# A transformer sandwich kernel: the adapter stage's normalisations moved from VectorE to ScalarE and GpSimd

## What is computed

```python
def _L1_ffn_ref(x, W, b, A, B, p_scores):
    z = jnp.einsum('bsd,od->bso', x, W) + b
    u = jnp.einsum('bsd,edr->ebsr', x, A)
    m = jnp.einsum('ebsr,ero,e->bso', u, B, p_scores)
    norm_z = jnp.linalg.norm(z, axis=-1, keepdims=True)
    norm_m = jnp.linalg.norm(m, axis=-1, keepdims=True)
    gamma = jnp.minimum(C_CLAMP * norm_z / (norm_m + EPS), 1.0)
    return z + gamma * m
...
x = x + _layernorm(_L1_ffn_ref(_layernorm(x, axis=-1), L1_ffn_W, L1_ffn_b, L1_ffn_A, L1_ffn_B, L1_ffn_p_scores), axis=-1)
```

## Time and profile before

| | us |
|---|---|
| median of 3 runs | 2067.3 (2067.06 to 2076.23) |
| profiled execution | 2061.47 |
| its span | 2059.7 |
| PE busy in the span | 1906.8 |
| DVE busy | 1405.4 |
| ACT busy | 1161.7 |
| POOL busy | 233.2 |

### The profile page before, as it was taken

How to read it: one execution, slowest core, us unless ns; L and a number is a source line. 1 busy time by engine, 2 the same in 40 slices (tenths; PEclk the granted TensorE clock), 3 DMA queues, 4 the chain that set the end, 5 groups by cost and what they waited for, 6 DMA issues and landing times. The chain is left out here.

```text
span 2059.7 us, 31844 instructions
## 1 busy us (share of the span) xinstructions
PE 1906.8 (93%) x11664; PEld 1079.1 (52%) x11664; DVE 1405.4 (68%) x2438; ACT 1161.7 (56%) x2422; POOL 233.2 (11%) x284
## 2 busy tenths in 40 slices
PE   6999999999999999989999999399999999999784
PEld 4875333333333333368888888264444444444563
DVE  5346999999998999465334231567777777773677
ACT  3223878888887888744222221124777777776443
POOL 0000000110000000250011010100001110003513
PEclk9999999999999999999999999699999999999998
DMA  6592454435444451143010100463534543431201
GB/s 210 159 194 77 69 83 86 77 70 88 75 74 64 77 84 37 39 139 111 1 41 1 42 21 0 138 172 81 96 100 85 103 86 75 87 70 44 78 21 61
DMA packets 124572, 165.60 MB, mean 80 GB/s; under 512 B 49364, under 2 KB 59988, under 8 KB 124272
## 3 DMA queue, kind: packets, MB, share of 16 engines
q1 hardware_dynamic: 120080, 148.64, 33.0%
q0 software_dynamic: 4336, 14.93, 2.3%
HBM read 104.92 MB, written 58.06 MB: 79 GB/s over the span
## 5 line engine op out<-in xcount | busy, mean ns | idle before, releaser
L961 DVE TENSOR_REDUCE maxesB<-banksB 128x1 f32<-128x1024 f32 x512 | 601.6, 1215 | 86.7 <-PE banksB L1028 86.7
L911 ACT ACTIVATE probsB<-banksB 128x512 f32<-128x512 f32 x1024 | 529.6, 602 | 128.4 <-PE banksB L1039 128.2
L958 DVE CUSTOM_DVE_ANT_0 junkG<-banksG,rampG 128x896 bf16<-128x896 f32 (+7 forms) x512 | 367.7, 755 | 100.5 <-PE banksG L1028 94.7
L1039 PE MATMUL banksB<-q_stackB,k_stackB 50*128 50x512 f32 x1024 | 403.5, 471 | 4.4 <-ACT probsB L911 2.1
L911 ACT ACTIVATE probsG<-banksG 128x512 f32<-128x512 f32 (+3 forms) x768 | 326.0, 492 | 117.2 <-PE banksG L1050 65.7
L1028 PE MATMUL banksB<-k_stackB,q_stackB 48*128 48x512 f32 x1024 | 344.6, 442 | 4.0
L1039 PEld LDWEIGHTS banksB<-q_stackB,k_stackB 50*128 50x128 f32 x1024 | 166.8, 184 | 265.0 <-ACT probsB L911 231.3
L1039 PE MATMUL banksG<-q_stackG,k_stackG 54*128 54x512 f32 (+3 forms) x768 | 258.8, 413 | 22.0 <-ACT probsG L911 16.5
L1072 PE MATMUL banksB<-probsB,v_onesB 128*32 128x512 f32 x2048 | 274.2, 608 | 0.0
L1028 PE MATMUL banksG<-k_stackG,q_stackG 52*128 52x512 f32 (+3 forms) x768 | 247.9, 408 | 8.7 <-DVE maxesG L958 8.3
L1028 PEld LDWEIGHTS banksB<-k_stackB,q_stackB 48*128 48x128 f32 x1024 | 153.9, 185 | 86.0 <-DVE maxesB L961 75.1
(11 more groups left out here) (296 smaller groups left out, 2785.0 us busy)
## 6 DMA issues: line engine op xcount, KB each, us to landing
q_stackB<-q_parts SPq DMA_DIRECT2D x96, 128.0 KB
k_stackB<-k_parts SPq DMA_DIRECT2D x96, 128.0 KB
q_stackG<-q_parts SPq DMA_DIRECT2D x96, 128.0 KB
q_parts<-partsA SPq DMA_DIRECT2D x16, 512.0 KB, 4.0
k_parts<-partsA SPq DMA_DIRECT2D x16, 512.0 KB, 2.8
turns<-o_copyB SPq DMA_DIRECT2D x32, 256.0 KB, 2.2
q_parts<-partsF SPq DMA_DIRECT2D x16, 512.0 KB, 2.8
turns<-o_copyG SPq DMA_DIRECT2D x32, 256.0 KB, 3.1
```

What stands on the lines that cost most here:

```text
L911: act.activation(probs[:, (i % ring) * GH + h, first:HALF], st_ps[:, n % n_st, first:HALF], ACT.Exp).then_inc(st_used, 1)
L958: dve.tensor_tensor_reduce(junk[:, n % JUNK, 0:width], scores, ramp[:, SEQ - width:SEQ], 1.0, LOWEST, ALU.add, ALU.max, out).then_inc(maxe ...
L961: dve.reduce_max(out, scores, AX.X).then_inc(maxed, 1)
L1039: ins = pe.matmul(st_ps[:, n % n_st, first:HALF], kst[at, it % 3, h % kh, kt * P:(kt + 1) * P], qst[at, it % 3, half, h % GS, first:HALF], ...
```

## The change

Three things move, all in the adapter stage. The next block's normalisation goes from VectorE to ScalarE, as `Identity(rstd * x + shift)`; VectorE works out `shift = -mean * rstd` in one small operation; ScalarE does tiles 0 and 1 ahead of the block's tile loop and tiles 2 and 3 behind tile 0. The normalisation of the last block's result goes from VectorE to GpSimd, ahead of its adds, for blocks 0 to 2; block 3's stays on VectorE. VectorE waits for those normalisations before it writes new means.

```diff
@@ block_residual_stats
     dve.wait_ge(r.summed, TB * (nb + 1))
+    if nb:
+        dve.wait_ge(r.normed, TB * nb)
...
 def block_residual_apply(dve, r, nb):
-
+    block_residual_inverse(dve, r, nb)
+    block_residual_tiles(dve, r, nb)
+
+
+def block_residual_inverse(dve, r, nb):
     dve.wait_ge(r.rooted, nb + 1)
     dve.reciprocal(r.rstd[:, :], r.rstd[:, :]).then_inc(r.inverted, 1)
-    dve.wait_ge(r.inverted, nb + 1)
+
+
+def block_residual_tiles(engine, r, nb):
+    engine.wait_ge(r.inverted, nb + 1)
     for i in range(TB):
-        dve.tensor_scalar(r.tile(nb, i), r.tile(nb, i), r.mv[:, i, 0:1], r.rstd[:, i:i + 1],
+        engine.tensor_scalar(r.tile(nb, i), r.tile(nb, i), r.mv[:, i, 0:1], r.rstd[:, i:i + 1],
                           ALU.subtract, ALU.mult).then_inc(r.normed, 1)
@@ Adapter
     def gpsimd(self, pool, out):
         for nb in range(NB):
+            if nb < NB - 1:
+                block_residual_tiles(pool, self.r, nb)
             block_residual_add(pool, self.r, self.n, nb)
+
+    def norm_next(self, act, nb, tiles):
+
+        n = self.n
+        act.wait_ge(n.inverted, nb + 1)
+        act.wait_ge(n.turned, TB * nb)
+        for i in tiles:
+            act.activation(n.xn[:, i, :], n.block(nb)[:, i, :], ACT.Identity, bias=self.shift[:, i:i + 1],
+                           scale=n.rstd[:, i:i + 1]).then_inc(n.normed, 1)
@@ Adapter.scalar
                 norm_root(act, n, nb + 1)
+                self.norm_next(act, nb + 1, range(0, 2))
...
+                if i == 0 and nb < NB - 1:
+                    self.norm_next(act, nb + 1, range(2, TB))
@@ Adapter.vector
             if nb < NB - 1:
-                norm_apply(dve, n, nb + 1)
+                dve.wait_ge(n.rooted, nb + 2)
+                dve.reciprocal(n.rstd[:, :], n.rstd[:, :]).then_inc(self.inverse, 1)
+                dve.wait_ge(self.inverse, nb + 1)
+                dve.scalar_tensor_tensor(out=self.shift[:, :], in0=n.mv[:, :, 0], scalar=-1.0, in1=n.rstd[:, :],
+                                         op0=ALU.mult, op1=ALU.mult).then_inc(n.inverted, 1)
...
                 if i == 3 and nb:
-                    block_residual_apply(dve, r, nb - 1)
+                    block_residual_inverse(dve, r, nb - 1)
```

More of the change, by code:

```diff
@@ L1591, in __init__ @@
         self.shift = slack_sb(f"shift{tag}", [P, TB], F32)
+        self.inverse = sems("ln_inverse")
         self.w = Weights(lambda name, *a: (turn_sb if name.startswith("w_") else slack_sb)(name, *a), sems, tag,
```

## The result

The changed kernel takes 2080.88 us (median of 20 runs, 2072.82 to 2086.89) against 2069.63 us before (20 runs, 2059.84 to 2082.63): a ratio of 1.0046, 95% interval 1.0030 to 1.0062. That is 9.5 us by the ratio and 11.25 us between the medians, and above the forecast range of 2063 to 2078. The profiled execution has a span of 2081.8 us.

The account below looks back on a forecast made before the run. VectorE was taken as the adapter stage's busiest engine, its normalisations and once GpSimd's adds on the path. The terms -1.25 + 2.25 + 2.1 = +3.1 us, put on the median of 2067.3, gave 2070.4 us, range 2063 to 2078.

Parts of the forecast that it names:

- I take 0.80 us: GpSimd in the adapter stage: one normalisation of a tile was taken to cost 0.80 us.
- the bounds of 0.60 and 1.29: Range for GpSimd's normalisation: cast of a tile 0.60 us below, fastest two-input add 1.29 us above.
- the second rival: GpSimd's normalisation costs much more than an add, over 1.43 us; at 2.0 us +17, 2084 us; chance 0.08.
- I to Z: Statistics-ending reciprocal I(b) to first bias add Z(b+2), b the block: 9.5 us (was 9.62), then 9.27 (7.02), including 0.7 and 0.5 lost.
- I(0): Reciprocal ending block 0's statistics: expected at 1994.03 instead of 1995.18 us, with ScalarE's normalisations costed at nothing.
- Z to I stays 14.9: Block 2, first bias add to the next reciprocal ending a result's statistics: unchanged at 14.9 us.
- The last stretch: After I(2), block 3's reciprocal: joins and GpSimd's adds take turns, last statistics at about I + 11.4 against 9.27, +2.1 us.
- the first rival: Last stretch: joins are not held by GpSimd and end at I + 5.7; sum -2.6 us, 2063 to 2065; chance 0.10.
- The wait on y_normed: VectorE's new wait before writing means: met by older work, in the last block by GpSimd's normalisations at I + 3.7.
- MODIFY_POOL_CONFIG: New operation before GpSimd's first normalisation: lies in GpSimd's idle time until after block 0's reciprocal, so costs nothing.
- The third rival: Loading GpSimd's code is paid at block 0's first normalisation: 2071.7 us, or 2076.4 by the skill; chance 0.07.
- own slope of 11.5: Each 0.1 us more per GpSimd normalisation costs 0.4 at Z(2), 0.4 at Z(3), about 0.35 at the end.

Follow-up runs that it names:

- prices: The kernel before plus seven scratch operations run twice on GpSimd in its idle time as the adapter stage starts; stage 109.26 us against 105.75, one run.
- act_only: The changed kernel with the last result's normalisation left on VectorE, so only ScalarE's part moves; ratio to the kernel before 0.9989 (0.9965 to 1.0012).
- pool_only: The changed kernel with the next block's normalisation left on VectorE, so only GpSimd's part moves; ratio to the kernel before 1.0067 (1.0042 to 1.0093).
- three_tiles: The changed kernel with a third buffer for y, so the first bias add waits for older adds; ratio to the kernel before 1.0021 (1.0003 to 1.0039).
- act_three: act_only with a third buffer for the blocks' results; ratio to the kernel before 0.9985 (0.9965 to 1.0004).
- double_stats: The changed kernel with a second buffer for the result's means and roots; adapter stage 119.28 us against 118.94 in the changed kernel, one run.
- beside: The kernel before plus scratch adds, TENSOR_SCALARs or copies on GpSimd beside VectorE's joins, by block; adapter stage 114.45 us against 105.75, one run.

## Why the prediction was wrong

**The step that failed** is the term "I take 0.80 us" in what GpSimd gets and its price, and with it the bounds of 0.60 and 1.29. Measured: 2.08 us. The case stood there as the second rival, "at 2.0 us it is 3.1 + 13.8 = +17, 2084", with a chance of 0.08. It happened, at 2080.9; that this is near 2084 is in part luck, since the growth was 11.25 us and not 17, from a median before of 2069.6 and not 2067.3. What misled was the argument "with one tensor input it is nearer to the cast": prices shows a one-input tensor_scalar of one step at 1.50 us, above the two-input add at 1.30. Of the two reasons weighed in that rival, the pointers ("for it") turn out to be worth 0.1 or 0.2 us; the kind of operation, which wasn't weighed, makes the price. The Trainium skill, GPSIMD Engine Reference, has in section 3.1, Elementwise — side-by-side cycle accounting, 769 ns for 512 elements as the best of a tight loop; the shortest tensor_scalar here took 1499 ns. The upper bound was also no bound: an add is a different operation, so its duration bounds nothing from above.

**I to Z.** The mechanism was right (Z released by GpSimd's adds, one queue of four normalisations and four adds). By its own formula with 2.08 us and no loss to VectorE, 0.33 + 8.3 + 5.14 + 0.1 is 13.9 us, measured 13.60 and 13.56. The 0.7 and 0.5 us for VectorE's operations in between were not lost by GpSimd: its normalisations took 8.29 us for four and its adds 4.96. Here it was VectorE that waited, L1735 1.13 and 1.08 us instead of 0.69.

**ScalarE's part and I(0).** Right to 0.01 us for I(0) in the change (40.07 from the start, 40.08 forecast), and nothing of it showed on the path: act_only.

**Z to I stays 14.9.** It became 16.25, by matmuls at the lower clock level behind TensorE's waits. This 1.34 us was not in the sum. What cost it were the slow transposes and matmuls behind the wait of 3.04 us for the low parts: from the first transpose to the fourth bias add 5.36 us. pool_only, with an equally late Z and a wait of 3.08 us there, had the full clock behind it, took 4.01 us for the same and kept 14.90. three_tiles and act_only had slow matmuls that cost time, act_three had none. What decides the clock is open.

**The last stretch.** +2.49 against +2.1 forecast, a hit by number and not by mechanism. The joins, to be held to about I + 11.4, were done at I(2) + 6.0, as the first rival had it. They met normalisations and not adds, since at 2.08 us each GpSimd was not yet at its adds; beside shows that the one holds joins hardly and the other does. The time was lost in GpSimd's own queue instead: 9.66 us of normalisations, one stretched to 3.49, and then eight adds in a row, 10.52 us.

**The wait on y_normed** was said to be met in the last block by normalisations done at I + 3.7. They were done at I(2) + 9.9, and VectorE waited 1.56 us, yet double_stats shows that this costs nothing. For the results of blocks 1 and 2 it was met, as forecast. **MODIFY_POOL_CONFIG** ran at 1965.6, and 37.56 us of idle time followed: hidden, as forecast. The third rival did not come: GpSimd started 0.27 us after I(0), and in prices it started within 0.2 us of MODIFY_POOL_CONFIG itself. The Trainium skill, GPSIMD Engine Reference, section 2.1, Instruction dispatch, has some 6 us for a first call to new code; the rows of prices do not agree, with 0.2 us and a first operation of 2.10 us.

**Sum.** With 2.08 us the prediction's own slope of 11.5 gives 3.1 + 14.7 = +17.8; the stage grew by 13.19. Of the 4.6 us between, 4.1 are the last stretch, where each 0.1 us was to cost 0.35 but the joins went free; 1.0 and 0.8 are the two I to Z pieces (14.6 and 14.4 by that slope); the slow matmuls take 1.3 back. The prediction's sums at its bounds are slightly off its own slope: it gives +0.8 us at 0.60 and not +0.6, +8.7 at 1.29 and not +8.6, -4.2 and not -4.4 for the first rival at 0.60, and 0.4 less and not 0.3 at 769 ns; nothing hangs on this. The median grew by 11.25 us, and the interval reaches to 12.8; the stage of the one profile of before had no slow matmul and was likely on the short side, which is not shown by more profiles of it.

## What to carry to other kernels

An engine with idle time is not a cheap engine: before an operation is moved to GpSimd, measure that very operation there, by kind and steps, since a cast and an add of the same tile say little about it. When two stages of work share a queue and a third waits for its end, the buffer count and the unit of the wait matter as much as the durations: working and waiting tile by tile, with no operation faster, took 13.0 us off the stage. And a removed wait can be paid again if it had kept operations apart that hold each other: before it goes, look at what will then lie side by side.

## What the runs showed of the hardware

- On GpSimd, 128x512 f32: tensor_scalar of two steps 2.08 us, of one step 1.50 to 1.71; add of two tiles 1.30; multiplication with a broadcast column 1.04; copy 0.61.
- VectorE's scalar_tensor_tensor of two SBUF tiles, 0.75 us alone: 1.75 to 1.89 us beside GpSimd's adds, about 0.75 beside its TENSOR_SCALARs except one at 1.10, 1.09 to 1.19 beside its copies (beside). Its TENSOR_TENSOR of two SBUF tiles, 0.69 us alone, took 1.08 to 1.13 beside GpSimd's TENSOR_SCALARs (the change, prices). VectorE's TENSOR_SCALAR, 0.54 us alone, took 1.48 beside adds (the change) and 0.82 to 0.97 beside TENSOR_SCALARs (prices).
- A GpSimd TENSOR_SCALAR of 2.07 us stretched to 3.15 us beside four joins (beside), and to 3.49 beside joins in the change. The first one of the program started within 0.2 us of MODIFY_POOL_CONFIG and took 2.10 us (prices).
- TensorE's clock fell to its lower level (matmuls 0.63 us instead of 0.39) for some us in some blocks, also in prices, where the work of all engines but GpSimd was that of before. Behind a wait of 1.77 us it fell in act_only and not in the kernel before; behind one of 3.04 us it fell in the change, and behind one of 3.08 us it did not in pool_only.
